# Early pairs' last top product beside the last sums over d, and the top's input in two tiles

## The chip, the cores and the metric

The kernel runs on one core of one Trainium2 chip. The metric is device time in microseconds (us) of a whole execution; lower is better. The core has a matrix engine (TensorE, PE), three engines for elementwise work (VectorE is DVE, ScalarE is ACT, GpSimd is POOL), a sync engine that issues transfers (SP), and DMA queues that SP, ACT and POOL feed. Each engine works its own list of instructions in order; semaphores tie the lists together.

## The reference

Per sample, 32 rows of 16 floats are looked up (`e`, batch 512). Three layers of a compressed interaction network follow, each with 64 outputs per d, then sums over d, and a small dense network on top of them:

```python
x0 = xk = e                                     # (512, 32, 16)
for W in (W0, W1, W2):                          # W: (32, h, 64)
    xk = relu(einsum('bmd,bhd,mhk->bkd', x0, xk, W))
    outs.append(sum(xk, axis=2))                # the sums over d, 64 per sample
h = concatenate(outs + [dense_ctx], axis=1)     # (512, 3*64 + 16 = 208)
h = maximum(h @ W_top1 + b_top1, 0.0)           # 208 -> 512
h = maximum(h @ W_top2 + b_top2, 0.0)           # 512 -> 256
y = h @ W_top3                                  # 256 -> 1
```

## The kernel before

The batch is cut into nine pairs `p` of sample groups (16, 24, six times 32, 24 samples in each of the two halves `t` of the batch; `NP = 9`). For each pair and each layer `n` (0, 1, 2), DVE and POOL form the elementwise products of the two factors (`z_vector`, `z_pool`), and PE contracts them with the layer's weights (`side_by_side`, L659; 64 output rows for each half, into one PSUM bank `result`). ACT takes the maximum with zero out of PSUM into `x_sb` (`relu`, L415), and DVE or ACT sums that over d into `d_sums` (`sum_d`, L576 or L423). The order of all of it is written out by hand in `STAGES` and in the engines' functions; `last` is pair 8.

The dense network on top ("the top") is done in two pieces. The *early* piece is for pairs 0 to 6 (`EARLY = 7`, 2 x 200 = 400 columns), the *late* piece for pairs 7 and 8 (2 x 56 = 112 columns). The early piece is seven steps `early(k)` on PE, each followed by a step of the same number on ACT: k = 0 to 3 are the four blocks of 128 outputs of the first matrix (L711, two matmuls each), k = 4 and 5 the two blocks of the second (L717, four matmuls each), and k = 6, `early(N1 + N2)`, is the third, with one output row (L723, two matmuls). ACT's part of k = 6 is `y_out` (L474), which copies the row into `y_sb`, and SP then stores it (L319). These steps are laid between the matmuls of the last layers.

The late piece comes in `late_top1(0)` (the first 128 inputs of the first matrix, L769), which needs the sums of layers 0 and 1 alone, and `late_top1(1)` (the rest, L769), which needs the sums of layer 2 of pair 8. Then come the second matrix (L791) and the third (L795, L797). Between the last matmul of layer 2 of pair 8 and `late_top1(1)` lies a chain that PE has no part in: ACT's `relu(2, last)` (L415), DVE's sum over d (L576), and the copies of the sums into the top's input by ACT (`top_block`, L469) and DVE (L644). In that stretch the kernel before has PE run `busy(3, result[0])` (L741): three matmuls whose result nobody reads.

The top's input `top_in` is one tile of 128 partitions x (2 halves of the rows) x (2 halves of the batch) x 256 columns, in the space of a buffer `r0_forms` that is free by then (the profile calls it `r_forms`). Its dense rows come by one DMA on ACT's queue (L539). The early matmuls read columns 0 to 199 of each half of the batch, so 400 columns in two runs; the late ones 56 and 56. PE's `early(0)` waits until all seven loads of the top have landed (`top_loaded`) and ACT's six copies are made (`early_in_ready`).

## Time and profile before

| | |
|---|---|
| Time, median of three runs | 337.7 us |
| Lowest and highest of them | 336.69 and 337.79 us |
| The profiled execution's own time | 335.4 us |
| Its span (first to last instruction) | 333.5 us |
| PE busy | 301.6 us, 90% of the span |
| DVE busy | 266.1 us, 80% |
| POOL busy | 246.3 us, 74% |
| ACT busy | 144.3 us, 43% |

The profiled execution is a single one. Its span leaves out 1.9 us of its own time, which lie around the first and the last instruction. PE's busy time includes the drain of a matmul, so a matmul that starts right behind another overlaps it; the distance from start to start tells what a group occupies. A float32 matmul appears as two records.

### The profile page before, as it was taken

Reading aid. Unit: us, or ns where it says so; the run is one execution under the profiler, and the core shown is the slowest. Engines: PE = TensorE matmul, PEld = TensorE weight load, DVE = VectorE, ACT = ScalarE, POOL = GpSimd, SP = SyncE. Lnnn points to the kernel's source line nnn. Section 1 sums busy time; section 2 is a strip of 40 time slices with the busy share of each in tenths; the row PEclk is TensorE's granted clock in tenths of the full one; section 3 lists DMA queues with packets and bytes.
Section 4 is the critical chain, followed back from the end, with each engine's and each line's share of the span. In section 5 each row is a group of like instructions: output and inputs, shape, how many; then the busy total and the mean of one; then the engine's idle time right before and its main releaser. Section 6 shows DMA issues by size and latency. Waiting matters only on the chain.

```text
span 333.5 us, 4735 instructions
## 1 busy us (share of the span) xinstructions
PE 301.6 (90%) x1498; PEld 115.1 (35%) x1498; DVE 266.1 (80%) x117; ACT 144.3 (43%) x862; POOL 246.3 (74%) x162
## 2 busy tenths in 40 slices
PE   0078787998999999999999999999999999999996
PEld 0044332453234333323333333333333334333444
DVE  0025939998999999999999999999999988971301
ACT  1001210316617724593489248824971386213012
POOL 5777777786888977897879797978892996938000
DMA  6286978969744996289838963795177502300000
GB/s 188 34 266 118 335 187 243 362 121 332 307 77 106 260 353 120 73 274 390 169 87 255 365 100 85 245 374 123 48 199 280 135 25 67 94 2 0 0 0 2
DMA packets 55169, 56.72 MB, mean 170 GB/s; under 512 B 37894, under 2 KB 43912, under 8 KB 51944
## 3 DMA queue, kind: packets, MB, share of 16 engines
q1 hardware_dynamic: 42088, 40.87, 37.7%
q10 hardware_dynamic: 8960, 14.49, 16.3%
q0 software_dynamic: 4096, 1.06, 3.2%
q8 instruction: 12, 0.20, 0.2%
q14 instruction: 13, 0.11, 0.1%
HBM read 41.33 MB, written 2.10 MB: 130 GB/s over the span
## 4 chain that ended last, share of the span: by engine, by line
PE 76%; DVE 12%; DMA 5%; issue 3%; POOL 2%; ACT 1%; SPq 0%; ACTq 0%; DVEq 0%
PE result L659 67%; DVE z_vector L603 6%; DVE z_vector L610 5%; PE left L696 2%; POOL gathered_rows L334 2%; DMA r_forms<-x_rows 2%; PE y_psum L741 1%; DMA xj_forms<-x_sb 1%; PE result L711 1%; PE y_psum L711 1%; PE result L717 1%; PE y_psum L717 1%; DMA gathered_rows<-table,row_index 1%; DMA x_rows<-gathered_rows 1%; DMA table_base<-base 1%
## 5 line engine op out<-in xcount | busy, mean ns | idle before, releaser
L659 PE MATMUL result<-z_vector,w_sb 128*64 128x512 f32 (+2 forms) x1064 | 209.8, 542 | 9.8 <-DVE z_vector L610 5.7
L603 DVE TENSOR_TENSOR z_vector<-left,r_forms 128x4096 f32<-128x4096 f32 (+3 forms) x44 | 168.3, 3868 | 10.4 <-PE left L696 8.0
L334 POOL DMA_INDIRECT gathered_rows<-table,row_index x128 | 121.4, 949 | 37.5 <-issue 35.1
L350 POOL TENSOR_TENSOR z_pool<-r_forms,xj_forms 128x2048 f32<-128x2048 f32 (+2 forms) x29 | 124.2, 4308 | 20.2 <-DMA xj_forms<-x_sb 13.8
L659 PEld LDWEIGHTS result<-z_vector,w_sb 128*64 128x64 f32 x1064 | 75.4, 137 | 137.8 <-issue 110.9
L610 DVE TENSOR_TENSOR z_vector<-left,r_forms 128x2048 f32<-128x2048 f32 (+3 forms) x52 | 90.1, 1788 | 22.5 <-DMA r_forms<-x_rows 18.5
L423 ACT ACTIVATE x_sb<-x_sb 128x16 f32<-128x16 f32 x360 | 71.5, 200 | 6.4 <-issue 6.4
L423 ACT ACTIVATION_READ_ACCUMULATOR x_sb<-x_sb 128x1 f32 x360 | 67.3, 187 | 0.0
L659 PE MATMUL result<-z_pool,w_sb 128*64 128x512 f32 (+2 forms) x232 | 49.9, 570 | 0.0
L415 ACT ACTIVATE x_sb<-result 128x512 f32<-128x512 f32 (+2 forms) x27 | 14.8, 549 | 64.8 <-PE result L659 52.9
L396 ACT ACTIVATE left<-xj_forms 128x512 f32<-128x512 f32 (+2 forms) x36 | 18.6, 545 | 30.9 <-DMA xj_forms<-x_sb 12.8
L741 PE MATMUL y_psum<-w_sb 128*64 128x256 f32 x56 | 14.6, 418 | 18.3 <-DMA x_rows<-gathered_rows 18.3
L576 DVE TENSOR_REDUCE d_sums<-x_sb 128x32 f32<-128x512 f32 (+2 forms) x15 | 8.9, 596 | 24.6 <-ACT x_sb L415 24.6
L659 PEld LDWEIGHTS result<-z_pool,w_sb 128*64 128x64 f32 x232 | 15.9, 137 | 32.1 <-issue 31.7
L387 ACT ACTIVATE left<-h_form 128x512 f32<-128x512 f32 (+2 forms) x18 | 10.0, 553 | 36.1 <-DVE z_vector L610 21.0
L741 PEld LDWEIGHTS y_psum<-w_sb 128*64 128x64 f32 x56 | 8.2, 152 | 24.2 <-issue 21.1
L464 ACT ACTIVATE left<-xj_form 128x512 f32<-128x512 f32 (+2 forms) x18 | 9.3, 546 | 10.1 <-DVE z_vector L603 8.0
L390 ACT ACTIVATE z_square<-h_form 128x512 f32<-128x512 f32 (+2 forms) x18 | 10.2, 568 | 0.0
L696 PE MATMUL left<-x_sb,select_sb 64*128 64x512 f32 (+2 forms) x32 | 8.4, 601 | 1.2 <-ACT x_sb L415 1.2
L659 PE MATMUL result<-z_square,w_sb 128*64 128x512 f32 (+2 forms) x36 | 8.8, 545 | 0.0
L696 PEld LDWEIGHTS left<-x_sb,select_sb 64*128 64x128 f32 x32 | 2.4, 185 | 6.5 <-issue 5.2
L488 ACT ACTIVATE r_forms<-result,b_top_sb 128x400 f32<-128x400 f32 x2 | 1.2, 596 | 7.9 <-PE result L711 7.9
(41 smaller groups left out, 46.2 us busy)
## 6 DMA issues: line engine op xcount, KB each, us to landing
r_forms<-x_rows SPq DMA_DIRECT2D x24, 1024.0 KB, 8.0
r_forms<-x_rows SPq DMA_DIRECT2D x8, 768.0 KB, 5.9
xj_forms<-x_sb ACTq DMA_DIRECT2D x24, 256.0 KB, 8.2
h_form<-x_rows SPq DMA_DIRECT2D x12, 256.0 KB, 3.9
xj_form<-x_sb ACTq DMA_DIRECT2D x12, 256.0 KB
gathered_rows<-table,row_index POOLq DMA_INDIRECT x128, 3.2
r_forms<-x_rows SPq DMA_DIRECT2D x4, 512.0 KB, 5.5
x_rows<-gathered_rows SPq DMA_DIRECT2D x24, 64.0 KB, 3.1
```

The lines of the kernel that those rows point to most:

```text
L334: nc.gpsimd.indirect_dma_start(gathered_rows[:, half % GATHERED, g], None, table, bass.IndirectOffsetOnAxis(ap=row_index[:, at:at + 1], ax ...
L350: nc.gpsimd.tensor_tensor(z_pool[:, unit % NZP, :, :, 0:columns(p)], r_forms(q, p)[:, :, s0:s1], xj1_forms[form_buffer(n, p)][:, :, 0:colu ...
L387: nc.scalar.activation(left[:, 1, t, 0:columns(p)], h_rows, ACT.Copy).then_inc(left_copied, 1)
L390: nc.scalar.activation(z_square[:, t, 0:columns(p)], h_rows, ACT.Square).then_inc(z_square_ready, 1)
L396: nc.scalar.activation(left[:, 1, t, 0:columns(p)], xj1_forms[form_buffer(n, p)][:, t, 0:columns(p)], ACT.Copy).then_inc(left_copied, 1)
L415: nc.scalar.activation(x_sb[n][:, 0:columns(p)], result_of(n, p)[:, 0:columns(p)], ACT.Relu).then_inc(x_ready[n], 1)
L423: done = nc.scalar.activation(copied[:, rows], x_sb[n][:, rows], ACT.Copy, accum_out=d_sums[:, n, START[p] + b:START[p] + b + 1])
L603: nc.vector.tensor_tensor(z_vector[:, unit % NV, :, 0:s1 - s0, 0:columns(p)], left[:, bank, :, 0:columns(p)].unsqueeze(2).broadcast_to([12 ...
L610: nc.vector.tensor_tensor(z_vector[:, unit % NV, t, 0:s1 - s0, 0:columns(p)], left[:, bank, t, 0:columns(p)].unsqueeze(1).broadcast_to([12 ...
L659: done = nc.tensor.matmul(result_of(n, p)[K * t:K * t + K, 0:columns(p)], weights, z[:, t, 0:columns(p)], start=first, stop=last)
L696: done = nc.tensor.matmul(left[:, 0, t, 0:columns(p)], select_sb[K * t:K * t + K], x_sb[n - 1][K * t:K * t + K, 0:columns(p)], start=True, ...
L741: nc.tensor.matmul(bank[0:K, 0:4 * K], w0_sb[:, 0], w12_sb[:, 0, 0, 0:4], start=True, stop=True)
```

## The change

Three edits go together.

1. `early(N1 + N2)` moves on PE from behind POOL's part of the last layer to behind its last matmul, where `busy(3, result[0])` stood, and `busy(3, ...)` is gone. On ACT its partner, `y_out`, moves from ahead of `relu(2, last)` to behind the last `top_block`.
2. `top_in` becomes two tiles, one for the early pairs (400 columns) and one for the late (112), in which the columns that a matmul reads lie in one run. Together they are as large as the one before (4 x 200 + 4 x 56 = 1024 floats per partition), so what lies behind them in the buffer stays where it was.
3. The dense rows come by two DMAs in place of one, and the waits on `top_loaded` count to 16 * 8.

```diff
--- before.py
+++ after.py
@@ -164,7 +164,9 @@
             spare_at[0] += columns
             return spare[:, at:at + columns]
 
-        top_in = from_spare(2 * B).rearrange("p (f t c) -> p f t c", f=2, t=2)
+
+        top_in = {pairs: from_spare(4 * (START[pairs[1]] - START[pairs[0]])).rearrange("p (f t c) -> p f t c", f=2, t=2)
+                  for pairs in ((0, EARLY), (EARLY, NP))}
         hidden1 = from_spare(N1 * EARLY_COLUMNS).rearrange("p (k c) -> p k c", k=N1)
         hidden2 = from_spare(N2 * EARLY_COLUMNS).rearrange("p (k c) -> p k c", k=N2)
         late1 = from_spare(N1 * LATE).rearrange("p (k c) -> p k c", k=N1)
@@ -466,7 +468,7 @@
 
             def top_block(n, t, pairs, ready):
                 samples = slice(START[pairs[0]], START[pairs[1]])
-                nc.scalar.activation(top_in[K * (n % 2):K * (n % 2) + K, n // 2, t, samples],
+                nc.scalar.activation(top_in[pairs][K * (n % 2):K * (n % 2) + K, n // 2, t],
                                      d_sums[K * t:K * t + K, n, samples], ACT.Copy).then_inc(ready, 1)
 
             def y_out(pairs, bank):
@@ -536,13 +538,15 @@
 
             act.wait_ge(z_vector_ready, 2 * vector_after((2, EARLY - 1)))
             act.wait_ge(z_pool_ready, 2 * pool_after((2, EARLY - 1)))
-            act.dma_start(top_in[K:K + D, 1], dense).then_inc(top_loaded, 16)
+            for pairs in top_in:
+                act.dma_start(top_in[pairs][K:K + D, 1], dense[:, :, START[pairs[0]]:START[pairs[1]]]
+                              ).then_inc(top_loaded, 16)
             early_inputs()
             copy_xj1(2, last - 1)
             relu(1, last)
             load_xj0(2, last)
             load_xj1(2, last)
-            act.wait_ge(top_loaded, 16 * 7)
+            act.wait_ge(top_loaded, 16 * 8)
             early(0)
             copy_xj0(2, last)
             for k in range(1, N1):
@@ -553,12 +557,13 @@
                 act.wait_ge(x_summed[n], NP)
                 for t in range(2):
                     top_block(n, t, (EARLY, NP), late_in_ready)
-            for k in range(N1, N1 + N2 + 1):
+            for k in range(N1, N1 + N2):
                 early(k)
             relu(2, last)
 
             act.wait_ge(x_summed[2], NP)
             top_block(2, 0, (EARLY, NP), late_in_ready)
+            early(N1 + N2)
             act.wait_ge(late1_summed, 1)
             for k in range(N1 // 2):
                 nc.scalar.activation(late1[:, k], late1_psum[0][:, k], ACT.Relu,
@@ -641,7 +646,7 @@
             sum_d(2, NP - 1)
 
             dve.wait_ge(x_summed[2], NP)
-            nc.vector.tensor_copy(top_in[0:K, 1, 1, START[EARLY]:START[NP]],
+            nc.vector.tensor_copy(top_in[EARLY, NP][0:K, 1, 1],
                                   d_sums[K:2 * K, 2, START[EARLY]:START[NP]]).then_inc(late_in_ready, 1)
             dve.wait_ge(late1_summed, 2)
             for k in range(N1 // 2, N1):
@@ -699,7 +704,7 @@
 
             def early(k):
                 if k == 0:
-                    pe.wait_ge(top_loaded, 16 * 7)
+                    pe.wait_ge(top_loaded, 16 * 8)
                     pe.wait_ge(early_in_ready, 6)
                 if k == 1:
                     pe.wait_ge(x_ready[0], NP)
@@ -710,7 +715,7 @@
                     for half, rows in enumerate((128, K + D)):
                         done = nc.tensor.matmul(
                             bank[:, 0:EARLY_COLUMNS], w_top1_sb[0:rows, half, 128 * k:128 * k + 128],
-                            top_in[0:rows, half, :, 0:START[EARLY]], start=half == 0, stop=half == 1)
+                            top_in[0, EARLY][0:rows, half].rearrange("p t c -> p (t c)"), start=half == 0, stop=half == 1)
                 elif k < N1 + N2:
                     pe.wait_ge(early_ready, N1)
                     for n in range(N1):
@@ -768,7 +773,7 @@
                 for k in range(N1):
                     done = nc.tensor.matmul(
                         late1_psum[k // 2][:, k % 2], w_top1_sb[0:rows, half, 128 * k:128 * k + 128],
-                        top_in[0:rows, half, :, START[EARLY]:START[NP]], start=half == 0 and k % 2 == 0,
+                        top_in[EARLY, NP][0:rows, half].rearrange("p t c -> p (t c)"), start=half == 0 and k % 2 == 0,
                         stop=half == 1 and k % 2 == 1)
                     if half == 1 and k % 2:
                         done.then_inc(late1_summed, 1)
@@ -778,9 +783,9 @@
             early(0)
             layer(2, last - 1, {0: [lambda: early(1)], 1: [lambda: early(2)],
                                 "pool": [lambda: early(3)]})
-            layer(2, last, {0: [lambda: early(N1)], 1: [lambda: early(N1 + 1)], "pool": [lambda: early(N1 + N2), lambda: late_top1(0)]})
-
-            busy(3, result[0])
+            layer(2, last, {0: [lambda: early(N1)], 1: [lambda: early(N1 + 1)], "pool": [lambda: late_top1(0)]})
+
+            early(N1 + N2)
             late_top1(1)
             for m in range(N2):
                 for k in range(N1):
```

In the rows below, a line is `L<line> operation out<-in rows x columns xcount`; the line numbers of the changed kernel are two to five higher than those of the kernel before. `result<-z_vector` and `result<-z_pool` are matmuls of a layer, `y_psum<-r_forms` with one row is `early(N1 + N2)`, `left<-r_forms` are `late_top1` and the second matrix, `result<-w_sb` is `busy`.

PE, the end of the program, before:

```order
L717 MATMUL result<-r_forms,w_top_sb 128x400 x4
L659 MATMUL result<-z_pool,w_sb 64x384 x8
L723 MATMUL y_psum<-r_forms,w_top_sb 1x400 x2
L769 MATMUL left<-r_forms,w_top_sb 128x112 x4
L659 MATMUL result<-z_vector,w_sb 64x384 x8
L741 MATMUL result<-w_sb 64x256 x3
L769 MATMUL left<-r_forms,w_top_sb 128x112 x4
L791 MATMUL left<-r_forms,w_top_sb 128x112 x8
```

PE, the same place of the changed kernel:

```order
L722 MATMUL result<-r_forms,w_top_sb 128x400 x4
L664 MATMUL result<-z_pool,w_sb 64x384 x8
L774 MATMUL left<-r_forms,w_top_sb 128x112 x4
L664 MATMUL result<-z_vector,w_sb 64x384 x8
L728 MATMUL y_psum<-r_forms,w_top_sb 1x400 x2
L774 MATMUL left<-r_forms,w_top_sb 128x112 x4
L796 MATMUL left<-r_forms,w_top_sb 128x112 x8
```

The two matmuls with one output row have moved behind the layer's last eight, and stand where the three unread ones stood.

ACT, the end of the program, before (`r_forms<-y_psum` and `r_forms<-result` are the early piece's steps, `x_sb<-result` is `relu`, `r_forms<-d_sums` is `top_block`, `h_form<-y_psum` is `y_out` of the early piece, `r_forms<-left` are the late piece's steps):

```order
L469 ACTIVATE r_forms<-d_sums 64x56 x4
L491 ACTIVATE r_forms<-y_psum,b_top_sb 128x400
L491 ACTIVATE r_forms<-result,b_top_sb 128x400
L474 ACTIVATE h_form<-y_psum 1x2x200
L415 ACTIVATE x_sb<-result 128x384
L469 ACTIVATE r_forms<-d_sums 64x56
L564 ACTIVATE r_forms<-left,b_top_sb 128x112 x2
```

ACT, the same place of the changed kernel:

```order
L471 ACTIVATE r_forms<-d_sums 64x56 x4
L493 ACTIVATE r_forms<-y_psum,b_top_sb 128x400
L493 ACTIVATE r_forms<-result,b_top_sb 128x400
L417 ACTIVATE x_sb<-result 128x384
L471 ACTIVATE r_forms<-d_sums 64x56
L476 ACTIVATE h_form<-y_psum 1x2x200
L569 ACTIVATE r_forms<-left,b_top_sb 128x112 x2
```

`y_out` now stands between the last `top_block` and the first step that reads the late piece's first matrix.

ACT, where the top's input is brought in, some 50 us ahead of the end, before (`left<-xj_form` and `left<-xj_forms` are copies for DVE's products):

```order
L437 DMA xj_forms<-x_sb 128x1x512 x2
L464 ACTIVATE left<-xj_form 128x512 x2
L539 DMA r_forms<-dense 16x512
L469 ACTIVATE r_forms<-d_sums 64x200 x6
L396 ACTIVATE left<-xj_forms 128x512 x2
```

ACT, the same place of the changed kernel:

```order
L439 DMA xj_forms<-x_sb 128x1x512 x2
L466 ACTIVATE left<-xj_form 128x512 x2
L542 DMA r_forms<-dense 16x2x200
L542 DMA r_forms<-dense 16x2x56
L471 ACTIVATE r_forms<-d_sums 64x200 x6
L398 ACTIVATE left<-xj_forms 128x512 x2
```

One DMA has become two, ahead of the six copies into the early tile.

## Rows read from the trace of the kernel before

**Rows 1.** The page: engines' busy time, and the last chain by engine.

```profile
PE 301.6 (90%) x1498; PEld 115.1 (35%) x1498; DVE 266.1 (80%) x117; ACT 144.3 (43%) x862; POOL 246.3 (74%) x162
...
PE 76%; DVE 12%; DMA 5%; issue 3%; POOL 2%; ACT 1%; SPq 0%; ACTq 0%; DVEq 0%
```

**Rows 2.** The chain that ended last, in order: start, us, what.

```profile
320.49 1.43 PE y_psum L723 x4
...
325.78 0.50 ACT x_sb L415
...
326.30 0.56 DVE d_sums L576
...
326.89 0.26 ACT r_forms L469
```

**Rows 3.** Timeline of PE, 314:334: start, us, what xrecords [idle <-releaser].

```profile
317.69 2.80 PE L659 MATMUL result<-z_pool,w_sb 128*64 128x384 f32 x16
320.42 1.50 PE L723 MATMUL y_psum<-r_forms,w_top_sb 128*1 128x400 f32 x4
321.85 1.15 PE L769 MATMUL left<-r_forms,w_top_sb 128*128 128x112 f32 x8
322.93 2.80 PE L659 MATMUL result<-z_vector,w_sb 128*64 128x384 f32 x16
325.56 1.46 PE L741 MATMUL result<-w_sb 128*64 128x256 f32 x6
327.19 1.15 PE L769 MATMUL left<-r_forms,w_top_sb 80*128 80x112 f32 x8 [0.17 <-ACT r_forms L469]
328.33 2.06 PE L791 MATMUL left<-r_forms,w_top_sb 128*128 128x112 f32 x16
```

**Rows 4.** Timeline of ACT, 319:334.

```profile
321.96 0.49 ACT L474 ACTIVATE h_form<-y_psum 1x400 f32<-1x400 f32 x1 [3.57 <-PE y_psum L723]
...
327.93 0.60 ACT L564 ACTIVATE r_forms<-left,b_top_sb 128x112 f32<-128x112 f32 x2 [0.79 <-PE left L769]
```

**Rows 5.** Timeline of PE, 321.8:323.0: the last record of L723.

```profile
321.43 0.50 PE L723 MATMUL y_psum<-r_forms,w_top_sb 128*1 128x400 f32 x1
```

**Rows 6.** Timeline of SP, 321:334: the two stores of y.

```profile
322.48 9.62 SPq L319 DMA_DIRECT2D y<-h_form  x2
```

**Rows 7.** Timeline of ACT and its DMA queue (ACTq), 274:297.

```profile
275.98 1.21 ACTq L437 DMA_DIRECT2D xj_forms<-x_sb  x2
...
277.45 1.02 ACTq L539 DMA_DIRECT2D r_forms<-dense  x1
...
278.52 2.34 ACT L469 ACTIVATE r_forms<-d_sums 64x200 f32<-64x200 f32 x6
280.88 1.12 ACT L396 ACTIVATE left<-xj_forms 128x512 f32<-128x512 f32 x2
286.22 0.49 ACT L415 ACTIVATE x_sb<-result 128x384 f32<-128x384 f32 x1 [4.22 <-PE result L659]
```

**Rows 8.** DMA issues: KB each, median us from issue to landing.

```profile
w_top_sb<-w_top SPq DMA_DIRECT2D x1, 512.0 KB, 12.3
...
r_forms<-dense ACTq DMA_DIRECT2D x1, 32.0 KB, 3.1
```

**Rows 9.** Timeline of PE, 274:297: the start of `early(0)`.

```profile
286.10 1.61 PE L711 MATMUL y_psum<-r_forms,w_top_sb 128*128 128x400 f32 x4
```

**Rows 10.** Timeline of DVE, 262:297.

```profile
280.46 8.74 DVE L603 TENSOR_TENSOR z_vector<-left,r_forms 128x4096 f32<-128x4096 f32 x2
```

**Rows 11.** Single lines: a record's ns, min/median/max, first and last start.

```profile
L711 PE MATMUL y_psum<-r_forms,w_top_sb x8: 497/500/604, 286.1 to 297.5; 128*128 128x400 f32 x4, 80*128 80x400 f32 x4
...
L717 PE MATMUL y_psum<-r_forms,w_top_sb x8: 499/499/604, 309.2 to 311.6; 128*128 128x400 f32 x8
...
L741 PE MATMUL y_psum<-w_sb x56: 378/379/660, 18.3 to 66.8; 128*64 128x256 f32 x56
```

**Rows 12.** Busy time by stretch; behind POOL: granted TensorE clock, DMA share, GB/s.

```profile
327.19:328.33 1.14, 1.14 (x8) 0.96 (x8) 0.00 (x0) 0.41 (x2) 0.00 (x0) 1.00 0.05 14
```

## Prediction

> **What bounds the kernel now.** I read the shares of busy time first. PE is busy for 90% of the span and makes up 76% of the chain that ended last [rows 1]. A share says nothing of a stage, so I read the chain in order of time next, and its end in particular. Up to ACT's piece at 325.78 us its last pieces are matmul groups, and the third product of the early piece, 1.43 us, is one of them [rows 2]. PE's timeline shows the same from the engine's side: the groups at 317.69, 320.42, 321.85, 322.93 and 325.56 us follow each other with no idle time in brackets [rows 3]. So until 325.56 us PE is the bound, and whatever is taken off its list there brings the end forward by as much.
>
> Behind that the bound changes. The chain leaves PE: ACT's maximum 0.50 us from 325.78, DVE's sum 0.56 from 326.30, ACT's copy 0.26 from 326.89, and only then `late_top1(1)` at 327.19 [rows 2, 3]. From the start of the unread matmuls (325.56) to `late_top1(1)` it is 1.63 us, and PE has no useful work in it. The unread products fill 1.46 us of it, and PE was idle for 0.17 us waiting for ACT's copy [rows 3]. The reader should see a hole of 1.63 us in which a group of 1.43 us might lie.
>
> **The move on PE.** Distances are from start to start, since that is what a group occupies. Before, L723 takes 321.85 - 320.42 = 1.43 us [rows 3]. Its removal moves `late_top1(0)` and the last eight matmuls of the layer earlier by 1.43 us. Nothing there holds them back: all groups behind it run back to back now [rows 3], and `late_top1(0)` needs only the sums of layers 0 and 1, whose copies on ACT stand ahead of two steps of the early piece and ahead of `y_out` at 321.96 [rows 4], in ACT's own order. The last layer group takes 2.63 us (322.93 to 325.56) ahead of another group of the same width, and 2.73 us (317.69 to 320.42) ahead of one of another width [rows 3]. So 0.10 us is the price of a change of width. Before, there was one ahead of L723; after, there is one ahead of `late_top1(0)` in the same place, so this cancels.
>
> The time line after then is: `late_top1(0)` at 320.42, the last layer group at 321.50, its end where the unread matmuls would start at 325.56 - 1.43 = 324.13, and L723 at 324.23 with the change of width. PE is free for the next group 1.43 us later, at 325.66. The chain ACT, DVE, ACT starts from the layer's last matmul, which has not changed, so `late_top1(1)` is released at 327.19 - 1.43 = 325.76. PE is free 0.10 us before that. The product is hidden, by 0.10 us. If that cover were gone, each 0.1 us too much would cost 0.1 us. The removal of the unread matmuls is worth nothing by itself, since PE waited behind them [rows 3].
>
> One price can be checked with notes on the chip. The Trainium skill (FP8 and Floating Point Precision, TensorE Precision Notes) says that a float32 matmul takes four passes, and (TensorE: Matmul & The Clock Gate, Back-to-back issue gap) that a pass at full clock takes columns / 2.4 + 2.5 ns. By these pages two matmuls of 400 columns take 2 x 4 x 169 ns = 1.35 us, and the sum below would be 0.08 us smaller. The case's own record starts give (321.43 - 320.42) / 3 = 0.337 us for each of the four records [rows 3, 5], hence 1.35 us, and the other 0.08 us is the change of width ahead of the next group. I take 1.43, as both leave together.
>
> **The move on ACT.** `y_out` started 1.54 us after L723 did (320.42 to 321.96) and took 0.49 us [rows 3, 4]. After, it starts at 324.23 + 1.54 = 325.77 and ends at 326.26. What is queued behind it is L564, the first step that reads the late first matrix, and PE's second matrix (L791) waits for that. L564 was released at 327.93 [rows 4], so now at 326.50. Slack 0.24 us, cost 0. Ahead of it, `top_block` would run at 325.46 to 325.72, and `y_out` stands behind it in the list, so it delays nothing there. ACT also no longer has `y_out` ahead of the maximum, but it had ended 3.3 us before that, worth 0.
>
> **The store of y.** SP's first store is issued at 322.48, the second near the end of the 9.62 us [rows 6]. The first moves to some 326.3 us, the second to 332.10 - 0.6 - 1.43, some 330 us. One issue takes 0.6 us (two take 1.21) [rows 7], and a small load took 3.1 us to land [rows 8], less than the 3.7 us between the two stores. Cost 0.
>
> **The split load.** One issue of the dense rows held ACT's queue for 1.02 us; two other issues together took 1.21 us, so one of them 0.6 [rows 7]. The second issue thus costs ACT 0.6 to 1.02 us. It sits ahead of six copies and two more for DVE; these shift to an end at 283.0 us at worst (280.88 + 1.12 + 1.02), and ACT then idles until 286.22, when PE releases it [rows 7]. `early(0)` starts on PE at 286.10 and its copies are made at 281.9 at the latest [rows 7, 9]. The two copies for DVE end by 283.0; DVE's third unit of the pair is the first that reads them, and its first two occupy DVE until 289.2 [rows 10]. The second transfer, issued by 278.47, would land at 281.6 with the 3.1 us of the one transfer now [rows 8]. That leaves 4.5 us to 286.10. Cost 0, as long as a landing takes less than 7.6 us.
>
> **Columns in a row.** Does a matmul get faster when its 400 columns are one run? The trace has both forms with equal width: L711 reads two runs of 200 and its records last 500 ns, L717 reads one run and its records last 499 ns [rows 11]. For 112 columns, L769 reads two runs, 1.15 / 8 = 0.144 us a record; L791 reads one, 2.06 / 16 = 0.129 [rows 3]. Both times hold one drain at the end, which weighs more on eight records than on sixteen, so most of the 15 ns is that. Bounds: 0 (by L711) to 16 x 0.015 = 0.24 us gained (by L769, both calls). I take 0, because L711 and L717 are the cleaner pair. A loss is excluded: one run is what L717 already has.
>
> **The sum.** 0 - 1.43 (L723 off the path) + 0 (unread matmuls) + 0 (`y_out`) + 0 (store) + 0 (load) + 0 (columns) = -1.43 us. The profiled execution, 335.4 us, would become 334.0. That execution lies 2.3 us below the median of the three runs shown and below their lowest; the difference has nothing to do with the tail, so I put the 1.43 us on the median: 337.7 - 1.43 = 336.3 us, 0.42% less. About 0.3%, 1.0 us, is what a measurement of this kernel can tell from no change.
>
> **Rivals.**
>
> *A, the forecast (0.82).* The product is hidden in the hole: 1.3 to 1.65 us gained, the upper end with the bound for the columns; 336.3 us.
>
> *B, the product fills the hole and more (0.11).* The cover on PE is 0.10 us and the one on ACT 0.24 us, both thin. If PE gets free of the product one record of 0.50 us [rows 5] later than worked out, `late_top1(1)` starts 0.40 us late, L564 is released at 326.90, and `y_out` has ended at 326.76: 336.7 us. If the next group also had to wait until `y_out` has ended, 0.5 us more, 337.2 us. If the product were wholly in series with the stretch, its 1.43 us would be back and the time 337.7, the change not doing what it says. For it speaks only the thinness. Against it speaks that `late_top1(0)` started 0.42 us after the start of L723's last record, inside its 0.50 us [rows 3, 5].
>
> *C, the second load comes late, the slower side (0.03).* Place: PE's wait ahead of `early(0)` at 286.10. A load of weights on SP's queue took 12.3 us to land [rows 8]. A landing of 12.3 us from 278.47 is 290.8, PE waits 4.7 us, and the time is 337.7 - 1.4 + 4.7 = 341.0 us. The wait begins at a landing of 7.6 us, and at 9.1 it has eaten the whole gain. Against it: that transfer is 16 times as large as the dense rows, which took 3.1. The Trainium skill (DMA: Bandwidth & Descriptors, Specifications) wants at least 512 bytes a descriptor and says that smaller ones cost a read-modify-write; the late piece's runs are 56 floats, 224 bytes. By this page the second transfer is of the slower kind, and the landing could exceed the 3.1 us of the first; no run here has shown it yet.
>
> *D, PE's matmuls get slower in the tail (0.02).* The unread products keep the array at work, and a product with one output row takes their place. The granted clock reads 1.00, the 2.4 GHz level, behind them now [rows 12]. Early in the kernel, records of L741 took up to 660 ns against 379 [rows 11], a factor of 1.74. On 1.14 + 2.06 us of tail this adds 2.4 us, so 338.7 us; it decides the sign from 1.43 us, that is from a factor of 1.45. Against it: PE is as full in time as before, 1.35 us of work against 1.46, and the idle time ahead of `late_top1(1)` stays near 0.1 us.
>
> *E, the columns in a row pay more than the bound (0.02).* The early records shorten too, 335.5 us or less.
>
> **From the cases to the numbers.** The forecast is case A. Its own size is sure within 0.2 us; the spread of runs is more: 336.69 to 337.79 before, and a profiled one at 335.4. Moving the first two by 1.43 gives 335.3 to 336.4; a low end of 335.0 adds the bound for the columns, and a high end of 337.5 takes in most of B. C, D and the upper part of B stay out. Faster by over 0.3%: nine tenths of A, E, and a little of B, 0.77. Within: the rest of A and most of B, 0.18. Slower: C and D, 0.05.
>
> **What would show it.** The product's row would stand at some 324.2 us with 1.50 us, with `late_top1(1)` within 0.1 us of its end and 1.63 us behind the layer's last matmul, as before. `y_out` would stand between L471's copy and L569, with L569 still 0.74 us behind the start of `late_top1(1)`. PE would have no idle time ahead of `early(0)`. The records of L716 would stay at 500 ns and those of L774 at 275. The prediction is wrong if the distance from the layer's last matmul to `late_top1(1)` grows by over 0.4 us, if PE waits ahead of `early(0)`, or if the time behind `late_top1(1)` grows.

## The result and the profile after

| | before | changed |
|---|---|---|
| Median of six runs | 337.66 us | 334.05 us |
| Lowest and highest | 335.42 and 337.85 us | 333.44 and 334.39 us |
| Profiled execution, its span | 335.4, 333.5 us | 334.32, 332.3 us |

The ratio of the changed kernel to the kernel before is 0.9906, 95% interval 0.9879 to 0.9934: it is faster by 3.6 us in the medians. Forecast were 336.3 us and a range of 335.0 to 337.5, so the change went the way that was forecast, by 2.5 times the 1.43 us forecast, and the time lies below the range. The interval of the ratio is wide in microseconds: 2.2 to 4.1 us. The two profiled executions, however, differ by 1.1 us only. The question of the study was which of these two figures belongs to the change.

The page of the changed kernel, busy time by engine and the last chain by engine:

```profile
PE 300.9 (91%) x1492; PEld 114.4 (34%) x1492; DVE 266.0 (80%) x117; ACT 144.4 (43%) x862; POOL 246.3 (74%) x162
...
PE 73%; DVE 13%; DMA 5%; issue 4%; POOL 2%; ACT 1%; SPq 0%; ACTq 0%; DVEq 0%
```

PE's timeline at the end, which answers to [rows 3]:

```profile
317.94 2.80 PE L664 MATMUL result<-z_pool,w_sb 128*64 128x384 f32 x16
320.68 1.15 PE L774 MATMUL left<-r_forms,w_top_sb 128*128 128x112 f32 x8
321.75 2.80 PE L664 MATMUL result<-z_vector,w_sb 128*64 128x384 f32 x16
324.48 1.50 PE L728 MATMUL y_psum<-r_forms,w_top_sb 128*1 128x400 f32 x4
326.01 1.15 PE L774 MATMUL left<-r_forms,w_top_sb 80*128 80x112 f32 x8
327.15 2.06 PE L796 MATMUL left<-r_forms,w_top_sb 128*128 128x112 f32 x16
```

From the layer's last group to `late_top1(1)` it is 326.01 - 321.75 = 4.26 us, and before it was 327.19 - 322.93 = 4.26 [rows 3]. The product sits in the hole and the hole has not grown. Between POOL's group and the last group lies 3.81 us (317.94 to 321.75) where it was 5.24 (317.69 to 322.93): the 1.43 us have gone from there.

ACT's timeline at the end, which answers to [rows 4]:

```profile
325.71 0.25 ACT L471 ACTIVATE r_forms<-d_sums 64x56 f32<-64x56 f32 x1 [0.62 <-DVE d_sums L581]
326.02 0.49 ACT L476 ACTIVATE h_form<-y_psum 1x400 f32<-1x400 f32 x1
326.75 0.60 ACT L569 ACTIVATE r_forms<-left,b_top_sb 128x112 f32<-128x112 f32 x2 [0.23 <-PE left L774]
```

`y_out` ends at 326.51 and ACT then idles for 0.23 us until PE releases L569. The slack of 0.24 us was there. (The prediction has `y_out` at 325.77; set back by the 0.26 us by which this execution's `early(0)` is later, it stands at 325.76.)

ACT and its queue where the top's input comes in, which answers to [rows 7], and the landings of the two DMAs:

```profile
277.71 1.05 ACTq L542 DMA_DIRECT2D r_forms<-dense  x1
...
278.79 0.66 ACTq L542 DMA_DIRECT2D r_forms<-dense  x1
279.50 2.33 ACT L471 ACTIVATE r_forms<-d_sums 64x200 f32<-64x200 f32 x6 [0.83 <-issue]
281.86 1.12 ACT L398 ACTIVATE left<-xj_forms 128x512 f32<-128x512 f32 x2
286.48 0.49 ACT L417 ACTIVATE x_sb<-result 128x384 f32<-128x384 f32 x1 [3.50 <-PE result L664]
...
DMA to landing us min/median/max: 2.3/2.6/3.0
```

The second issue cost ACT 0.7 us (idle 0.83 for issue; 4.22 us of idle time before, 3.50 now ahead of L417), and both transfers landed within 3.0 us, well ahead of `early(0)` at 286.36. The second, whose runs are 224 bytes long, took 2.3 us for its 7 KB, the first 3.0 us for its 25 KB; rival C's late landing didn't come. The records of the matmuls that now read one run are as long as before [rows 11]:

```profile
L716 PE MATMUL y_psum<-r_forms,w_top_sb x8: 497/500/603, 286.4 to 297.7; 128*128 128x400 f32 x4, 80*128 80x400 f32 x4
```

So each step in the profile came out as the prediction had it. What did not was the distance between the profile and the other runs. A profile can be cut in two at the start of `early(0)`: the *head* ahead of it, 286.10 us before and 286.36 in the changed kernel, and the *tail* from there to the end of the span, 47.40 and 45.94 us. The tail shows a gain of 1.46 us; the head is 0.26 us longer, although the only edited instructions in it are ACT's two DMA issues and its six copies into the new tile, in its last 9 us.

### The profile page after: what moved, and what is told of

It reads as the page before. It is cut to its first block, busy times and chain, and to the rows that moved or that the text cites. A ratio compares the mean times of both kernels' runs of the same rounds, so it can differ in the third digit from the quotient of the medians.

```text
span 332.3 us, 4724 instructions
## 1 busy us (share of the span) xinstructions
PE 300.9 (91%) x1492; PEld 114.4 (34%) x1492; DVE 266.0 (80%) x117; ACT 144.4 (43%) x862; POOL 246.3 (74%) x162
## 4 chain that ended last, share of the span: by engine, by line
PE 73%; DVE 13%; DMA 5%; issue 4%; POOL 2%; ACT 1%; SPq 0%; ACTq 0%; DVEq 0%
PE result L664 65%; DVE z_vector L608 8%; DVE z_vector L615 5%; POOL gathered_rows L336 2%; PE left L701 2%; DMA xj_forms<-x_sb 2%; DMA r_forms<-x_rows 1%; PE y_psum L746 1%; PE result L716 1%; PE y_psum L716 1%; PE result L722 1%; PE y_psum L722 1%; DMA x_rows<-gathered_rows 1%; DMA gathered_rows<-table,row_index 1%; PE left L774 1%
## 5 line engine op out<-in xcount | busy, mean ns | idle before, releaser
L417 ACT ACTIVATE x_sb<-result 128x512 f32<-128x512 f32 (+2 forms) x27 | 14.9, 551 | 66.8 <-PE result L664 50.2
```

What stands on the lines that cost most here:

```text
L417: nc.scalar.activation(x_sb[n][:, 0:columns(p)], result_of(n, p)[:, 0:columns(p)], ACT.Relu).then_inc(x_ready[n], 1)
```

## The experiments

Sixteen kernels ran in four sets, e1 to e4, e5 to e8, e9 to e12 and e13 to e16. The kernels of a set ran on one chip, a different one for each set, beside 33 to 35 runs of the kernel before. "Tail" is read from each kernel's one profile, "lowered" counts runs whose mean granted TensorE clock over the span is 0.9965 or less. Six runs took far longer than the rest (375.7, 415, 657, 1128, 1132 and 1811 us); they have no trace, and the means, the fits and the counts for the kernel before leave them out. The interval is that of the ratio; one that holds 1 shows no difference.

| Run | median, us | before beside it | ratio, 95% interval | tail, us | lowered |
|---|---|---|---|---|---|
| e1 same | 335.83 | 336.26 | 1.0009 [0.9974, 1.0044] | 47.38 | 3 of 12 |
| e2 move only | 334.90 | | 0.9967 [0.9937, 0.9997] | 45.96 | 5 of 12 |
| e3 tiles only | 336.12 | | 0.9987 [0.9951, 1.0023] | 47.41 | 5 of 12 |
| e4 changed | 333.56 | | 0.9914 [0.9879, 0.9949] | 45.99 | 0 of 10 |
| e5 no unread | 356.55 | 356.26 | 1.0 [0.9964, 1.0036] | 47.38 | all |
| e6 move, split | 354.31 | | 0.9948 [0.9918, 0.9977] | 45.95 | all |
| e7 late in two runs | 353.94 | | 0.9937 [0.9909, 0.9966] | 45.99 | all but the one of 1128 us |
| e8 early in two runs | 353.70 | | 0.9942 [0.9914, 0.9969] | 45.95 | all |
| e9 one unread more | 355.07 | 356.91 | 0.9933 [0.9907, 0.9959] | 46.41 | all but the one of 1811 us |
| e10 no product | 356.09 | | 0.9963 [0.9927, 0.9998] | 47.52 | all |
| e11 changed | 354.48 | | 0.9939 [0.9904, 0.9974] | 45.98 | all |
| e12 move only | 355.05 | | 0.9953 [0.9921, 0.9986] | 45.94 | all |
| e13 same | 335.96 | 336.32 | 1.0001 [0.9968, 1.0033] | 47.39 | 4 of 12 |
| e14 changed | 334.31 | | 0.9947 [0.9921, 0.9974] | 45.99 | 4 of 13 |
| e15 head filled | 334.73 | | 0.9943 [0.9914, 0.9971] | 46.00 | 2 of 12 |
| e16 tiles only | 335.87 | | 0.9996 [0.996, 1.0032] | 47.45 | 5 of 12 |

### One part of the change at a time

e1 is the kernel before, unchanged, and e4 the changed kernel. e2 has edit 1 alone, e3 has edits 2 and 3 alone. On PE, e2 differs from the kernel before in the lines below, and e3 from the changed kernel in the same lines the other way round; on ACT `y_out` goes with them. Dots stand for the rest of a line:

```diff
-            layer(2, last, {... "pool": [lambda: early(N1 + N2), lambda: late_top1(0)]})
-            busy(3, result[0])
+            layer(2, last, {... "pool": [lambda: late_top1(0)]})
+            early(N1 + N2)
```

> The kernel before, unchanged, under another name. Six runs of it lay at 337.6 to 337.9 (four), 336.7 and 335.4 us (one each), and the profiled one, at 335.4, was among the low ones. Theory of two levels: ratio 1.000, and its runs fall again into a level near 337.7 and one near 335.4, some 2.3 us apart, so the kernel before loses about 2.3 us in most executions somewhere that the profile of the low one does not show; a profile that falls on a high one would have a span near 335.7 instead of 333.5. Theory of drift (the runs before were simply noisy): a continuous spread of 335.4 to 337.9.

> Edit 1 alone: the third product of the early piece stands in place of the unread ones; one tile and one DMA as before. Theory M (the move gives all): 334.0 us, ratio 0.990, like the changed kernel. Theory L (the move gives its 1.43 us, and the tiles or the split DMA remove the other 2.2 us, which most runs of before have): 336.2 us, ratio 0.996, with the same spread as before. In both, the tail of the profile is 1.43 us shorter.

> Edits 2 and 3 alone: two tiles, two DMAs of dense; the third product and the unread ones stay where they were. Theory M: 337.7 us, ratio 1.000. Theory L: 335.5 us, ratio 0.9935, and hardly a run near 337.7.

> The changed kernel once more, beside the same runs of the kernel before as the three others. Both theories: ratio 0.990, runs within 333.4 to 334.4 us. If the level of before is a matter of the chip and not of the kernel, the ratio here is 0.996, with both at the same level.

The tails are 47.38 and 47.41 us without the move, 45.96 and 45.99 with it. The move is worth 1.43 us in the profile, the tiles nothing. In the medians e2 gained 1.4 us and e4 2.7; e3 gave 0.1. Neither theory fits the 2.7, since the parts don't add up to it. The theory of two levels fell too: 32 runs of before spread from 334.8 to 340.3 us, in which 22 lie at clock 0.999 or 1.000 (334.8 to 336.5 us), six at 0.995 (336.7 to 339.1) and four at 0.990 (339.5 to 340.3). So runs differ by a few us of lowered clock, and e4 had none in ten. (That is ten lowered runs; the expectations of e5 speak of 11 of 33.)

One more source of spread stands in e3's own profile, at clock 1.00 and with a span of 335.4 us. Its chain has a load of 9.39 us in the middle of the head, and DVE waited for it. The first line is of the chain, the second of DVE's timeline:

```profile
181.09 9.39 DMA r_forms<-x_rows
...
190.50 2.29 DVE L614 TENSOR_TENSOR z_vector<-left,r_forms 128x2048 f32<-128x2048 f32 x1 [2.28 <-DMA r_forms<-x_rows]
```

This profile shows the old order in a run of 337.48 us, near the median of the first set: the head is 287.99 us, 1.9 us longer than in the profile before, and the tail is the usual 47.41.

### Is the lowered clock tied to the tail or to the columns

```diff
 e5: before, and
-            busy(3, result[0])
 e6: edit 1, and two DMAs into the one tile
+            for samples in (slice(0, START[EARLY]), slice(START[EARLY], START[NP])):
+                act.dma_start(top_in[K:K + D, 1, :, samples], dense[:, :, samples]).then_inc(top_loaded, 16)
 e7, e8: changed, the late or the early tile with one float left free behind each half of the batch
-                        top_in[EARLY, NP][0:rows, half].rearrange("p t c -> p (t c)"), ...
+                        top_in[EARLY, NP][0:rows, half], ...
```

The last two lines are e7's; e8 has the same for the early tile. In both, the output of the late piece's second matrix (`late2`) also moves to the start of the buffer.

> The kernel before without its three unread products, so that PE is idle from the layer's last matmul to the last quarter of the late piece's first matrix, about 1.9 us. About a third of the runs of before have a mean granted clock of 0.995 or 0.990 and are 2 or 4 us longer than the rest. Theory T (the clock falls in the tail, and the tail's activity decides it): more runs with a lowered clock than the 11 of 33 of before, half or more, and a profile that falls on one shows the granted clock at 0.5 between 320 us and the end, with the records of the late piece twice as long. Theory U (it falls somewhere upstream, the tail has no part in it): the same share as before, a third, and the runs with clock 1.000 are as long as those of before, 334.8 to 336.5 us. Theory Z (the unread products are worth nothing): the same as U.

> The move and the two DMAs of the dense rows, with the one tile of before, so that matmuls still read their columns in two runs. The changed kernel had no lowered clock in 16 runs, the move alone in 5 of 12. Theory R (columns in a row remove the falls): some 4 or 5 of 12 runs with a lowered clock, median 334.7. Theory S (the split load, by moving something in time): none, median 333.6. Theory C (chance): none of the edits matters, something between. Runs at clock 1.000 in all cases 333.9 to 334.2 us.

> The changed kernel with the late tile's columns in two runs of 56 again (a float is left free between them); the early tile has its 400 in a row. Theory R1 (the late matmuls' columns in a row remove the falls): lowered clock in a third of the runs, median 334.3 or more. Theory R2 (it is the early ones): none, median 333.6, like the changed kernel. In runs at clock 1.000 no difference over 0.2 us, by the bound of 15 ns a record.

> The changed kernel with the early tile's columns in two runs of 200 again; the late tile has its 112 in a row. Theory R1: none with a lowered clock, median 333.6. Theory R2: lowered clock in a third of the runs. In runs at clock 1.000 no difference, since the records of L711 and L717 are equal.

This chip gave all runs, those of before too, a head some 20 us longer and a mean clock of 0.966 to 0.986, so shares of lowered clocks could not tell R from S here. Yet it showed where a clock can fall. PE's timeline of e8 in the head, and busy time by stretch with the granted clock as the third figure from the end:

```profile
31.85 1.22 PE L705 MATMUL left<-x_sb,select_sb 64*128 64x256 f32 x4 [4.27 <-ACT x_sb L421]
...
57.41 1.65 PE L705 MATMUL left<-x_sb,select_sb 64*128 64x384 f32 x4 [8.01 <-ACT x_sb L421]
```

```profile
28.00:31.00 3.00, 0.00 (x0) 0.00 (x0) 0.00 (x0) 0.00 (x0) 0.57 (x1) 0.92 0.34 73
31.00:33.00 2.00, 1.15 (x4) 0.53 (x4) 0.00 (x0) 0.38 (x1) 0.00 (x0) 0.50 0.86 133
...
57.00:60.00 3.00, 2.59 (x7) 1.12 (x8) 0.72 (x1) 0.36 (x1) 0.00 (x0) 0.50 0.91 176
```

PE idles for 4.3 and 8.0 us while ACT is late with two of its first maxima, and the clock is at 0.50, the 1.2 GHz level, right behind. That ACT is late there is in the trace, why it is has no row. Theory T, that the tail alone decides, has fallen by this. R and S, by which columns in a row or the split load would remove the falls, fall with e14 below, which has both and a lowered clock in 4 of 13 runs. The tails settle the columns: 45.99 and 45.95 us with two runs in the late or in the early tile, 45.95 with one tile and two DMAs. Columns in a row are worth nothing in the tail. And e5's tail of 47.38 us says that the unread products of the kernel before gave nothing in that execution (its `early(0)` starts at 305.12, so `late_top1(1)` stands 41.09 us behind it, to the hundredth as before); PE idled in their place:

```profile
346.21 1.15 PE L769 MATMUL left<-r_forms,w_top_sb 80*128 80x112 f32 x8 [1.46 <-ACT r_forms L469]
347.35 2.06 PE L790 MATMUL left<-r_forms,w_top_sb 128*128 128x112 f32 x16
```

### How well the product fits the hole

```diff
 e9: changed, and
             early(N1 + N2)
+            busy(1, result[0])
             late_top1(1)
 e10: changed, PE without
-            early(N1 + N2)
```

e10 leaves the early piece's third product out, so 400 of the 512 outputs are not computed; ACT's copy and the store stay, but ACT no longer waits for the product.

> The changed kernel with one unread product (two records of 256 columns) behind the third product, ahead of the last late_top1. From early(0) to the end of the span the changed kernel took 45.94 to 45.99 us, those with the old order 47.38 to 47.41. If the cover of the product is the 0.10 us worked out, the unread one (about 0.43 us) puts late_top1(1) later by 0.33 to 0.43 us, and the stretch is 46.3 to 46.4 us. If the hole had more room (theory of a loose fit), 45.95 us.

> The changed kernel without the third product of the early piece on PE at all (400 of the 512 outputs are not computed; ACT's copy of the row and its store stay). If the product is wholly hidden in its new place, the stretch from early(0) to the end is that of the changed kernel, 45.95 us; if it costs something there, it is shorter by that, 0.1 us or more. PE is then idle for about 1.9 us ahead of the last late_top1; if that idle time made the clock fall in the tail, the stretch would be longer.

> The changed kernel a third time. Its time can be split at early(0): the stretch behind it 45.95 us, and the head ahead of it, which holds no edited instruction up to the first DMA of dense rows. Theory H (the rest of the measured gain is the spread of the head): the head of its runs has the spread of that of before on the same chip, and the difference of the medians is anything from -4 to +1 us with -1.4 in the middle; of its runs as large a share has a lowered clock as of before. Theory K (the changed program has a better head): no or hardly any run with a lowered clock where before has a third, and a difference of 2 us or more again.

> The move alone once more. Theory H: stretch behind early(0) 45.95 us, and a head with the spread of before. Theory K (it takes the tiles or the two DMAs as well): lowered clock as often as before, while the changed kernel beside it has none; a difference of 1.4 us to before against 2.5 or more of the changed kernel.

PE's timeline of e9:

```profile
345.12 1.50 PE L728 MATMUL y_psum<-r_forms,w_top_sb 128*1 128x400 f32 x4
346.55 0.65 PE L746 MATMUL result<-w_sb 128*64 128x256 f32 x2
347.13 1.15 PE L774 MATMUL left<-r_forms,w_top_sb 80*128 80x112 f32 x8
```

The product occupies 346.55 - 345.12 = 1.43 us, as taken; in the changed kernel `late_top1(1)` starts 1.53 us behind the product's start. The cover is 0.10 us. The one unread product more takes 0.58 us with the change of width and delays `late_top1(1)` by 0.48, a little more than the 0.33 to 0.43 expected; the tail grows by 0.43 (46.41 against 45.98 in e11), the upper end of what was expected. The theory of a loose fit is out.

e10 brought the mechanism of rival D, to which the prediction gives 0.02, though in a kernel whose hole is empty and not in the changed one. Its tail is not 45.95 but 47.52 us. PE's timeline and the stretches of it:

```profile
348.33 1.15 PE L774 MATMUL left<-r_forms,w_top_sb 80*128 80x112 f32 x8 [1.46 <-ACT r_forms L471]
349.47 3.65 PE L795 MATMUL left<-r_forms,w_top_sb 128*128 128x112 f32 x16
```

```profile
346.80:348.33 1.53, 0.07 (x3) 0.00 (x1) 0.74 (x2) 0.79 (x3) 0.00 (x0) 1.00 0.00 0
348.33:349.47 1.14, 1.14 (x8) 0.96 (x9) 0.00 (x0) 0.73 (x3) 0.00 (x0) 1.00 0.00 0
349.47:353.05 3.58, 3.58 (x18) 3.38 (x18) 0.58 (x2) 0.54 (x2) 0.00 (x0) 0.52 0.00 0
```

The second matrix took 3.65 us where it takes 2.06 at full clock. PE had been idle for 1.46 us; the granted clock still read 1.00 in the 1.14 us of `late_top1(1)` behind that and 0.52 in the stretch after it. The same idle time in e5 had no such sequel, so it differs from execution to execution. The Trainium skill (TensorE: Matmul & The Clock Gate, What's actually happening) says that the clock is released by how busy PE has been of late; e10's trace agrees, with 0.52 behind the idle stretch, and e5's shows no fall behind an equal one.

e10 also answers its own question. `early(0)` starts at 308.68 there and at 306.12 in e11, so `late_top1(1)` stands 39.65 us behind it in both: the product in the hole costs nothing. Without the 1.59 us of the slower second matrix the tail would be 45.93 us, that of the changed kernel.

Does the hole have to be filled at all? The runs don't settle it. In the medians e10, with less work than e11, is 1.6 us slower than it, but resampling the twelve runs of each gives an interval of -1 to 3.5 us; and e5, with its hole empty too, has the median of the kernel before (ratio 1.0, 0.9964 to 1.0036). All 16 profiles with a filled hole, by unread products or by the third product, have the second matrix at 2.06 us; of the two with an empty hole, e5 has that too and e10 does not. What the change saves is in any case the work that stood elsewhere.

### Does the changed kernel have a better head

```diff
 e15: changed, and unread products in three waits of the head
-                layer(1, p)
+                layer(1, p, {1: [lambda: busy(3)]} if p == 1 else {})
+                if p == 0:
+                    busy(3)
...
-                    busy(6)
+                    busy(8)
```

> The kernel before under another name again. Stretch from early(0) to the end 47.4 us if the clock holds in the tail, as in four of four profiles of the old order so far; 48.5 to 49.5 us if the clock falls there, which the theory of a falling clock in the old tail expects in about a third of executions. Median within 0.4 us of before.

> The changed kernel a fourth time. Stretch 45.95 us. Theory H (spread of the head): median 1.4 us below the two old ones beside it, give or take 0.8. Theory K (a better head): 2.3 us or more below, and fewer runs with a lowered clock. The share of each run's time that lies outside its span was 1.98 us in the mean for kernels with two DMAs of dense rows and 2.17 for before; this should show again: 1.9 to 2.05 against 2.15.

> The changed kernel with eight more unread products in three of PE's waits of the head (1.38 us at 40 us, 0.89 us at 49 us, 1.31 us at 56 us in the last profile at full clock): three, two and three. If lowered clocks come from PE's idle time in the head, fewer runs have one and the mean clock rises, by 0.002 or more; time lower by up to 1 us. If they come from stalls of ACT that no filling reaches, no change, or slower by 0.1 to 0.5 us where the products last longer than the wait.

> The tiles and the two DMAs alone, again. Stretch 47.4 us. If these edits give something of their own beside the 0.17 us outside the span, the median lies 0.4 us or more below the old ones beside it; else within 0.4 us.

e14 settles the head. Its profile is one of an execution with a mean clock of 0.990, 338.22 us long, of the changed kernel. PE's timeline of it, and DVE's:

```profile
38.11 1.95 PE L664 MATMUL result<-z_vector,w_sb 128*64 128x256 f32 x16 [0.32 <-DVE z_vector L615]
43.68 5.39 PE L664 MATMUL result<-z_vector,w_sb 128*64 128x384 f32 x16 [3.62 <-DVE z_vector L615]
```

```profile
41.87 1.76 DVE L615 TENSOR_TENSOR z_vector<-left,r_forms 128x1536 f32<-128x1536 f32 x1 [2.15 <-DMA r_forms<-x_rows]
```

The same places in e13, the kernel before on the same chip at clock 1.00:

```profile
41.67 2.80 PE L659 MATMUL result<-z_vector,w_sb 128*64 128x384 f32 x16 [1.77 <-DVE z_vector L610]
```

```profile
39.86 1.76 DVE L610 TENSOR_TENSOR z_vector<-left,r_forms 128x1536 f32<-128x1536 f32 x1 [0.30 <-DMA r_forms<-x_rows]
```

And the clock of e14 by stretch:

```profile
40.00:44.00 4.00, 0.38 (x4) 0.30 (x4) 1.76 (x1) 0.38 (x1) 2.87 (x4) 0.82 0.97 363
44.00:47.00 3.00, 3.00 (x12) 1.00 (x10) 0.00 (x0) 0.00 (x0) 2.39 (x3) 0.50 0.62 83
```

A load that lets DVE go 2.0 us later (41.87 against 39.86) makes PE idle for 3.62 us in place of 1.77; the clock is at 0.50 behind that, and the next 16 records take 5.39 us in place of 2.80. The head is 290.3 us against 285.5 in e13. All of it lies at 40 to 50 us, some 230 us ahead of the first edited instruction, and the tail of this execution is 45.99 us. The changed kernel had a lowered clock in 4 of 13 runs here, before in 10 of 34, so the changed program is not free of it. On the two slow chips the mean clocks are alike, 0.976 to 0.978 for e6, e7 and e8 against 0.978 for before, and 0.976 for both e11 and before. Theory K in its strong form, of a changed kernel with hardly a lowered clock, has fallen. A somewhat smaller share is neither shown nor ruled out: over the first comparison, e4 and e14 it is 4 of 29 runs, against 20 of 66 of before on the two fast chips.

e13 and e16 kept the tail of the old order, 47.39 and 47.45. e16's median is 0.1 us below e13's and 0.45 below that of before, with 1 well inside its interval. e15 is no gain: from two lowered runs of twelve (the one of 375.7 us among them) against four of thirteen nothing can be told, and its median is 0.4 us above e14's.

## Why the prediction was wrong in size

**Right: the move, 1.43 us.** The six profiles of the old order (before, e1, e3, e5, e13, e16) have a tail of 47.38 to 47.45 us, the ten with the move 45.94 to 46.00, those with an edit to the hole (e9, e10) left aside. The difference is the same whatever the head was. The cover of 0.10 us on PE (e9, e10) and 0.24 on ACT, the cost 0 of the removed unread products (e5), of the columns (e3, e7, e8), of the store and of the load's landing all came out as taken. Rivals B, C and E didn't come. D's mechanism exists, in e10, but in none of the profiles of the changed kernel.

**Wrong: the step from the profile to the runs.** The prediction put it as "the difference has nothing to do with the tail, so I put the 1.43 us on the median: 337.7 - 1.43 = 336.3 us", and took the low end of the range from the lowest of the three runs. The first half is borne out (e3's profile at 337.48 us and e14's at 338.22 have the tails of their order and long heads), and the second doesn't follow. If the 2.3 us between the profiled execution and the median were no property of the tail, they were spread of the head, and spread need not come again. Four of six runs of the first set of before lay at 337.6 to 337.9 us; the medians of before on the two like chips were then 336.3, with 20 of 66 runs at a lowered clock. The profiled execution, 335.4 us, was an undisturbed one: the runs of before at a clock of 0.999 or 1.000 on these chips have medians of 335.8 and 335.7 us. By it, 335.4 - 1.43 = 334.0 us, where the changed kernel measured 334.05 and later 333.56 and 334.31. The range should have reached down to it. That the two agree to 0.1 us is in part luck: all six runs of the changed kernel were at clock 1.00, which nothing in the program ensures.

**Missed: 0.17 us outside the span.** The time of a run less its span was 2.15 to 2.17 us in the mean in the four sets of before and 2.10 to 2.26 in e1, e2, e5, e12 and e13, all with one DMA of dense rows. It was 1.95 to 2.03 in the kernels with two (e10 alone had 2.10), e6 with its single tile among them. So it goes with the second DMA, not with the tile. It is no even shift: in the kernels with one DMA the single runs fall into two groups, 74 of 195 at 2.0 us or less and the others at 2.12 to 2.50, while all 122 runs of those with two, e10 aside, lie at 2.15 or less. Why is not shown.

**The account.** 1.43 us (move) and 0.2 (outside the span) are 1.6 us. A least-squares fit over 277 runs (the kernels without an edit to the hole or the head, and before; a few runs of over 370 us left out), with a level for each of the four chips, gives the kernels with the move 2.0 us less, standard error 0.2. On the two fast chips one can look at the undisturbed runs alone: over the 103 runs at a clock of 0.999 or 1.000 a fit with a level for each chip gives the move 1.46 us, standard error 0.17, which is what the tails say, and the tiles with the two DMAs 0.4 us, standard error 0.16, of which 0.17 is the time outside the span.

Of the first comparison's 3.6 us, 1.6 are thus traced. About 0.4 us more, up to the fit's 2.0, stay open: they may be chance, at two standard errors, a somewhat smaller share of lowered clocks, something of the two DMAs in the head, or a tail whose clock falls now and then in the old order, of which no profile shows one.

The last 1.6 us I put down to the head, by the levels that e4's and e14's neighbours show and by the clock of 1.00 in all six runs of the changed kernel. This part is argued and not shown. The runs of before near 337.7 have no trace themselves, their chip isn't on record, and they were unusual: of the 66 later runs 13 lay at 337.6 us or more, and by that share four or more of six would do so in one case of sixty. The first set may have had a level of its own.

## What to carry to other kernels

When PE waits for a short chain on other engines, and the wait is filled with products that nobody reads, look for a needed product that stands on the critical path elsewhere, that nothing waits for soon, and that is as long as the filling; its whole time comes off the path, here 1.43 us of 335. Size it by distances from start to start, the change of width included, because here 0.1 us more would already have counted.

Before a profile is set against a median, split it at the first edited stage. If the profiled execution lies away from the other runs, the spread has to have a place in the program; where it lies ahead of the edit, a forecast for another build goes from the undisturbed execution, with a range that holds both.

## What the runs showed of the hardware

- An idle PE of 3.6 us (e14), and in one execution of two one of 1.5 us (e10, not e5), was followed by a granted clock of half the level; 16 records of 384 columns then took 5.39 us in place of 2.80, and 16 of 112 columns 3.65 in place of 2.06.
- The same program took 336 us on two chips and 356 on two others, with a mean clock of 0.98 there; in the profile of e8, one of these, PE waited 4.3 and 8.0 us for two of ACT's first maxima. The profiles of the slow chips have heads of 304 to 309 us, against 285 to 290. Within one order of the last groups the tail was equal on all four to within 0.1 us, e10's fallen clock and e9's added product aside.
- Behind the same load DVE could start at 39.9 us in one execution (e13) and at 41.9 in another (e14), in a stretch where the two kernels are equal. The head was 4.8 us longer there, of which 2.6 us are the 16 slower records alone.
